# A feed-forward block of local attention and gated layers: two layers over two sequences, as four staggered passes with a guest of experts beside them

## What is computed

```python
def _layer(x, wqkv, qs, ksc, wo, lg, lb, w1, b1, w2, b2):
    h = shift_token(x)
    q, k, v = jnp.split(h @ wqkv, 3, axis=-1)          # 8 heads of 64
    q = l2norm(q) * qs
    k = l2norm(k) * ksc
    q, k = rotary_xpos(q, k)
    o = local_attention(q, k, v)                       # window 64
    x = x + o @ wo
    h = shift_token(x)
    h = (h - mu) / jnp.sqrt(var + 1e-05) * lg + lb
    a, g = jnp.split(h @ w1 + b1, 2, axis=-1)          # 341 hidden each
    x = x + (a * gelu(g)) @ w2 + b2
...
# _L1_ffn_ref: 64 experts of width 64, the 8 chosen of them weighted
h = silu(einsum('td,edf->etf', xf, W_up))
y = einsum('etf,efd->etd', h, W_down)
routed = einsum('etd,te->td', y, cw)
```

## Time and profile before

| what | value |
|---|---|
| time, median of 3 runs | 5565.12 us (5562.16 to 5575.62) |
| the profiled execution | 5573.75 us |
| its span | 5572.0 us |
| TensorE busy | 4237.3 us, 76% |
| VectorE busy | 3172.3 us, 57% |
| ScalarE busy | 2506.1 us, 45% |
| GpSimd busy | 1501.4 us, 27% |
| granted TensorE clock, mean | 0.879 |

### The profile page before, as it was taken

One profiled execution on the slowest core, in us unless ns is written; L12 is line 12 of the kernel. 1 busy time (PEld: TensorE's weight loads), 2 busy tenths in 40 slices (PEclk: granted clock), 3 DMA queues, 4 the chain that ended last, 5 costly groups with the idle time before them and its releaser, 6 DMA issues. The chain is left out here.

```text
span 5572.0 us, 51193 instructions
## 1 busy us (share of the span) xinstructions
PE 4237.3 (76%) x16034; PEld 2320.4 (42%) x16034; DVE 3172.3 (57%) x5382; ACT 2506.1 (45%) x5663; POOL 1501.4 (27%) x1096
## 2 busy tenths in 40 slices
PE   5686688787876878777886878768787787877756
PEld 3444444444533544344444434434443444444312
DVE  3323365765556555755557655575556655575576
ACT  2343344543454434634446444554346444464332
POOL 2102131531125112421215322251114312252111
PEclk7787798998998989989899889989899898999877
DMA  3020011210121110311103111121112111031122
GB/s 89 1 76 0 2 47 39 83 52 28 48 65 59 44 36 31 105 35 33 43 20 106 45 31 47 59 67 48 31 36 96 40 33 44 23 106 43 37 70 69
DMA packets 188817, 273.95 MB, mean 49 GB/s; under 512 B 23448, under 2 KB 102900, under 8 KB 188532
## 3 DMA queue, kind: packets, MB, share of 16 engines
q1 hardware_dynamic: 167652, 234.89, 13.4%
q10 hardware_dynamic: 20880, 35.52, 2.1%
HBM read 215.54 MB, written 54.79 MB: 49 GB/s over the span
## 5 line engine op out<-in xcount | busy, mean ns | idle before, releaser
L638 DVE SCALAR_TENSOR_TENSOR psum<-work,psum 128x512 f32<-128x512 f32 x528 | 366.6, 694 | 600.5 <-ACT work L576 599.4
L1463 POOL MEMSET work<- 128x256 f32 x32 | 10.0, 311 | 2323.8 <-POOLq L1265 1165.4
L1426 ACT ACTIVATE work<-psum,work 128x128 f32<-128x128 f32 (+1 forms) x1024 | 389.8, 393 | 421.6 <-DVE work L1523 421.4
L553 PE MATMUL psum<-work,w_up 128*128 128x512 f32 x1024 | 572.7, 643 | 1.5 <-DVE work L632 1.5
L558 PE MATMUL psum<-work,w_down 128*128 128x512 f32 x1024 | 551.9, 621 | 20.4 <-DVE work L645 18.2
L576 ACT ACTIVATE work<-psum 128x512 f32<-128x512 f32 x528 | 317.4, 601 | 345.2 <-PE psum L553 276.3
L1288 PE MATMUL psum<-ident,work 128*128 128x128 f32 x1024 | 187.1, 343 | 330.7 <-POOL work L1477 330.6
L1344 PE MATMUL psum<-work 128*128 128x64 f32 x3072 | 415.8, 291 | 0.0
L1344 PEld LDWEIGHTS psum<-work 128*128 128x128 f32 x3072 | 388.1, 204 | 39.0 <-issue 32.2
L1470 POOL TENSOR_TENSOR work<-work,minus_half 128x16 f32<-128x16 f32 x128 | 374.3, 2924 | 10.7
L645 DVE TENSOR_TENSOR work<-work,psum 128x512 f32<-128x512 f32 x512 | 351.4, 686 | 19.6 <-DMA work<-expert_weight_rows 2.1
(11 more groups left out here) (210 smaller groups left out, 8834.6 us busy)
## 6 DMA issues: line engine op xcount, KB each, us to landing
work<-expert_weight_rows SPq DMA_DIRECT2D x1024, 128.0 KB, 2.9
position_scores<-work SPq DMA_DIRECT2D x64, 768.0 KB, 3.5
work<-position_scores SPq DMA_DIRECT2D x64, 512.0 KB, 3.8
work<-state_readout_rows ACTq DMA_DIRECT2D x72, 256.0 KB, 3.4
cent<-state_readout_rows ACTq DMA_DIRECT2D x32, 256.0 KB, 3.6
sq<-state_readout_rows ACTq DMA_DIRECT2D x24, 256.0 KB, 3.6
rows<-in_L_attn_q SPq DMA_DIRECT2D x8, 256.0 KB, 3.7
expert_weight_rows<-work SPq DMA_DIRECT2D x16, 128.0 KB, 2.3
```

The costliest lines, as they stand in the source:

```text
L553: nc.tensor.matmul(UP, b.w_up[:, p * 128:(p + 1) * 128], self.xn, start=True, stop=True).then_inc(self.up, 1)
L638: v.scalar_tensor_tensor(out=UP, in0=self.tanh_h[p % self.turns][0:rows], scalar=1.0, in1=UP, op0=ALU.add, op1=ALU.mult).then_inc(self.sil ...
L1426: ins = s.activation(prob_of(u)[:, i, first:first + n], score_banks[:, i, first:first + n], ACT.Exp, bias=neg_max[:, t, 4 * half + i:4 * h ...
```

## The change

The two layers over two sequences become four passes (`LocalFfn`, `PASSES = DEPTH * GROUP_SEQS`): pass i is layer i // 2 of sequence i % 2. A pass has 5 rounds of projection, 8 of attention and 7 of mixing, and the rounds of neighbouring passes alternate on each engine: projection 0; attention 0 with projection 1; attention 1 with mixing 0; projection 2 with mixing 1; attention 2 with projection 3; attention 3 with mixing 2; mixing 3. I call these seven stretches A to G, and B4 is round 4 of B. All stand in one block. The guest gets 3, 5, 5, 7, 5, 5 and 8 steps in them. VectorE takes the step of a pair of experts one round after TensorE issued it. The guest's up products have one bank in place of two, and its step 2 is no longer issued in the norm block but in A.

```diff
@@ Experts @@
-    BESIDE = ((5, 6), 7)
+    BESIDE = ((6,), 7)
...
-        self.aff = bank(b, self.ups[1])[:, 0:TILES * EXPERTS].rearrange("p (t e) -> p t e", t=TILES)
-        self.norm_banks = self.ups[0:2]
+        self.aff = bank(b, self.sum_bank)[:, 0:TILES * EXPERTS].rearrange("p (t e) -> p t e", t=TILES)
+        self.norm_banks = (self.ups[0], self.sum_bank)
@@ norm_block, on TensorE, ScalarE and VectorE @@
-            beside.tensor(pe, upto=3)
@@ ffn_stage @@
-    for l in range(DEPTH):
-        ffn_layer(nc, b, prefixed(f"layer{l}"), l, beside, space, transfers if l == 0 else ([], None))
+    LocalFfn(nc, b, prefixed("passes"), space).run(beside, transfers)
@@ LocalFfn @@
+    def project_tensor(self, pe, i, k):
...
+        for n in (2 * k, 2 * k + 1):
+            out = bank(b, 4 + n % 2)
+            if 10 * i + n >= 2:
+                pe.wait_ge(self.evicted, 10 * i + n - 1)
+            if k < 3:
...
+                nc.tensor.matmul(out, b.xn[:, at:at + 128], b.wqkv[:, l, part * INNER:(part + 1) * INNER],
+                                 start=True, stop=True).then_inc(self.projected, 1)
+            else:
+                t, part = k - 3, n % 2
+                if part == 0:
+                    pe.wait_ge(self.rotated, 2 * i + t + 1)
...
+    def attend_tensor(self, pe, i, k):
+        if k == 0:
+            self.unit_scores(pe, i, 0)
+        elif k <= self.GROUPS:
+            m = k - 1
+            self.turn_probs(pe, i, m)
+            u = self.UNIT_OF[m]
+            if m in (0, 1, 2):
+                self.unit_scores(pe, i, u + 1)
+            if m >= 1:
+                self.values(pe, i, m - 1)
+        else:
+            self.values(pe, i, self.GROUPS - 1)
...
+    def attend_vector(self, dve, i, k):
+        if k == 0:
+            self.maxima(dve, i, 0)
+        elif k <= self.GROUPS:
+            m = k - 1
+            if m in (0, 1, 2):
+                self.maxima(dve, i, self.UNIT_OF[m] + 1)
+            if m % 2 == 1:
+                self.copy_probs(dve, self.nc.vector.tensor_copy, i, m, self.p_copied_v)
+            if m == 2:
+                self.scale_heads(dve, i, 0)
+        else:
+            self.scale_heads(dve, i, 1)
...
+    def run(self, beside, transfers):
+        P, A, M = self.PROJECT, self.ATTEND, self.MIX
+        due = lambda guests, k, n: (k + 1) * guests // n - k * guests // n
...
+                for k in range(A):
+                    self.attend_tensor(pe, 0, k)
+                    if k < P:
+                        self.project_tensor(pe, 1, k)
+                    beside.tensor(pe, due(5, k, A))
...
+                for k in range(A):
+                    self.attend_vector(dve, 0, k)
+                    beside.vector(dve, due(5, k - 1, A) if k else 0)
+                    if k in (1, 3):
+                        self.project_vector(dve, 1, k // 2)
...
+                for k in range(M):
+                    if k in (1, 3):
+                        self.project_vector(dve, 2, k // 2)
+                    beside.vector(dve, due(7, k - 1, M) if k else due(5, A - 1, A))
+                    self.mix_vector(dve, 1, k)
```

More of the change, by code:

```diff
@@ L1197, in _ @@
             norm.scalar(act, (0, 1), steps=(1,))
-            beside.scalar(act, upto=3)
         @block.vector
@@ L1204, in _ @@
             norm.vector(dve, dst, (0, 1), steps=(1,))
-            beside.vector(dve, upto=3)
 def ffn_stage(nc, b, stage_sem, beside, space, transfers):
@@ L1578, in _, with mix_scalar @@
-        @block.sync
-        def _(sp):
-            for dst, src in transfers[0]:
-                sp.dma_start(dst, src).then_inc(transfers[1], 16)
-            beside.sync(sp)
+                if c == 2:
+                    pe.wait_ge(self.gated, 3 * i + 3)
+                ins = nc.tensor.matmul(two[:, 0:SEQ], b.w2[0:rows, l, c], self.k_t[i % 2][0:rows, c], start=c == 0, stop=c == 2)
+            ins.then_inc(self.out, 1)
+    def mix_scalar(self, act, i, k):
+        s, b = self.nc.scalar, self.b
+        l, cols = self.where(i)
+        one, two = (bank(b, n) for n in self.mix_banks(i))
+        if k == 0:
+            act.wait_ge(self.o_turned, 2 * i + 1)
+            s.copy(self.o_t[:, :, 0:128], one.rearrange("p (j n) -> p j n", j=4)).then_inc(self.o_copied_a, 1)
+        elif k == 2:
+            act.wait_ge(self.centred, i + 1)
+            s.activation(b.sq[:, cols], two[:, 0:SEQ], ACT.Square).then_inc(self.h_squared, 1)
+        elif k == 3:
+            s.preload_act_table_set("natural_log_exp_and_others")
+            act.wait_ge(self.variance, i + 1)
+            s.activation(b.rstd[:, cols], one[:, 0:SEQ], ACT.Ln, bias=b.eps[:]).then_inc(self.logged, 1)
+            act.wait_ge(self.logged, i + 1)
+            s.activation(b.rstd[:, cols], b.rstd[:, cols], ACT.Exp, scale=-0.5).then_inc(self.inverse, 1)
+        elif k in (4, 5):
+            for c in ((0, 1), (2,))[k - 4]:
+                rows = HC[c][1]
+                act.wait_ge(self.hidden, 3 * i + c + 1)
+                s.activation(self.q_t[i % 2][0:rows, c], (one, two)[c % 2][0:rows, 0:SEQ], ACT.Gelu,
+                             bias=vec(b, (("b1_gate", c), l), rows)).then_inc(self.gelu, 1)
```

689 lines of the change are left out of this document (374 added, 315 removed).

## The result

The changed kernel takes 5725.47 us (median of 4 runs, 5717.88 to 5736.84). The kernel before, run beside it, took 5570.17. The ratio is 1.0282, with a 95% interval of 1.0256 to 1.0307. It is slower by 155 us.

A forecast was written before the change was run, and what follows sets the result against it. TensorE's work plus waits around GpSimd bounded 14 stages, mostly waits and half clock the two without a guest. +174 and -88 made +86 us on 5573.75, or 5660; with the runs' lower median 5650, range 5480 to 5800.

The forecast's parts named there:

- the likeliest case: Rival 1, as worked out: more waits in 14 stages than two give back; 5650 us, own range 5590 to 5730, chance 0.50.
- the half clock: TensorE at lower clock after waits: 1.8 us charged in B and E each, 1.0 in C and F each, 1.3 in D.
- 14 stages with a guest, without the front: Guest stages from first to last copy: 237.0 us each in place of 222.2, before the 2.4 us saved ahead.
- ahead of them, step 2 moved: Block boundary ahead of a guest stage, the front: guest's step 2 no longer holds it, 2.4 us less a stage.
- 2 stages without a guest: Same TensorE work and low clock, fewer waits: 199 us in place of 243.2, -88 us for two.
- E4: Round 4 of stretch E, not a run: as in B4, TensorE's second-tile transposes wait 5.2 us for GpSimd.
- 66 us of waits and half clock: Guest stage after the change: A 14, B and E 22.6, C and F 17.4, D 8.0, G 4, against 51 before.
- 171 us of work: TensorE's work at full clock in a guest stage: passes 110.8 us, 32 pairs 57.0, the rest about 3.
- The single bank: Round 7 waits for the pair because there is one up bank and VectorE is a round behind: 2.6 us.
- Faster: Rival 2: round 7 waits and half clock behind gaps do not come; stage 219 us, total 5400, chance 0.28.
- ScalarE late: Rival 3: loads and copies delay mixing's tanh and gelu 1.4 us at eight places; 11 us a stage, 5805, chance 0.12.
- No change: Rival 4: loss and gain cancel, with a stage of 229.7 to 232.1 us; chance 0.10.

The follow-up runs named there:

- Pair first: Changed kernel with VectorE's pair of experts ahead of the scaling of the heads in round 7 of B, C, E and F: 5559.45 us, ratio 0.9981.
- pairs away from the norm: Kernel with the three edits, the five pairs of C and of F moved to rounds 0, 1, 2, 6 and 7: 5565.45 us, ratio 0.9996.
- no lag: Changed kernel with VectorE's pair in the same round as TensorE's, at TensorE's place, not one round later: 5668.74 us, ratio 1.0159.
- three edits: Changed kernel with pair first, second tile's query/key transposes in round 6 of B and E, and their round 4 pair in round 5: 5438.55 us.
- pairs left D: Kernel with the three edits, D's pairs of rounds 1 and 3 moved to C and F: 5494.35 us, ratio 0.9847.
- the last kernel: Kernel with the three edits; in A, query sums on VectorE and guest step 2 behind the second tile's projection work: 5423.85 us, ratio 0.9734.

## Why the prediction was right

Predicted was 5650 with a range of 5480 to 5800 and 0.62 for slower; 5725 is in the range, and by 5 us in the own range of the likeliest case. The mechanism was right: each wait stands where the order in the code put it. One term of the sum, the half clock, measured twice its forecast or more, and waits that came out shorter than forecast hid much of that. In the profiled execution the terms came out so:

| term | forecast | measured |
|---|---|---|
| 14 stages with a guest, without the front | 14 x +14.8 = +207 | +271 (222.2 to 241.6 in the mean) |
| ahead of them, step 2 moved | 14 x -2.4 = -34 | -26 (gaps between the blocks' parts, 15 of them) |
| 2 stages without a guest | -88 | -91 |
| the rest | 0 | +3 |
| sum | +86 | +157 |

- **Where the waits are.** Forecast in B4 and E4 5.2 us for GpSimd, measured 5.42; in round 7 of B, C, E and F 2.6, measured 2.35; in D 1.8, 3.3 and 0.5, measured 1.60, 3.14 and 0.51; in C and F 1.5, 1.5, 1.2 and 0.9, measured 1.31, 1.29, 1.44 and 0.46. The 1.1 for GpSimd in D4 did not come, G has 2.5 in place of 4, and rounds 0 to 3 of B and E have 0.4 to 1.1 in place of 1.7.
- **The mis-sized term** is the half clock within the 66 us of waits and half clock in a stage with a guest. Taken against the same 171 us of work, the 66 us measured 68.8 and 72.3. A is 2.1 us of that in either stage: 24 forecast, 26.1 measured. I had costed the chain from VectorE to GpSimd, and not that VectorE's comparison L618 would be held up beside GpSimd's product (below); by the timeline 1.7 of the 2.1 us are that, which no run isolates. B to G were forecast at 45.1 us of waits and 6.9 of half clock. They have 38.1 us of waits and 14.6 of the rest in the first-block stage, 38.0 and 18.3 in the third-block one (their length less the waits and less 161 us of work, which is the 171 without A's 10), at a clock of 0.94 and 0.92. So the waits were 7 us too long and the half clock 8 to 11 too short. That the sum for the first-block stage came so close is luck in that part. I charged 1.8 us behind B4 and 1.0 in C, and the up product alone lost 1.06 at 2085.20. Pair first shows the price of a short wait: 7.6 us fewer of them in round 7 brought 5.9 us less busy time as well.
- **First block and third block.** The third block's stage is 4 us longer in the changed kernel, and all of it is TensorE's slower work: it is busy for 192.87 us against 188.92 with the same 856 instructions, while the waits of B to G are equal. What gives the third block the lower clock is open.

```profile
1716.40:1959.70 243.30, 192.87 (x856) 120.38 (x856) 139.72 (x254) 111.72 (x264) 55.27 (x34) 0.89 0.11 36
```

- **The stages without a guest** came at 193.2 and 199.7 against 199.
- **Tables.** ScalarE's busy time in a stage went from 99.4 to 111.4 us. The seven more loads are 9.0 us of that, as forecast (14 loads in the window, 18.0 us, against 7 and 9.0); the other 3.0 come with 13 activations and 4 copies more. The Trainium skill's drain of about 1.38 us per load (ScalarE: Activation LUTs, What ACT_TABLE_LOAD costs) is not in the traces: the activation starts 0.02 us behind the load, and the load 0.02 us behind the one before it (the tanh from 2071.43 is 0.60 us long, the next load starts at 2072.05). Taking 13 loads away gave 6.3 to 9.1 us a stage, a third to a half of their 1.28 us each. The Trainium skill's advice to batch by set (ScalarE: Activation LUTs, Table sets: the hidden batching unit) does hold here, since 122 us hang on the loads. But the run with the pairs away from the norm shows that batching which takes cover away loses.
- **The single bank** I named as one half of the reason for round 7, and that is not shown. It cost nothing in the kernel before, and in the changed one the down product behind would have waited for the same pair. What the runs show as the cause is the lag together with the order, in which the pair stands behind an instruction that waits for TensorE's last values: without the lag (no lag), or with the lag and the pair ahead of the scaling (pair first), the wait is 0.44 us in place of 2.35, each time with one bank.
- **The other cases.** *Faster* needed the round-7 waits and the clock behind them to be missing. They came. With them taken out by hand the kernel is at 5559, level with the one before and not at the 5400 of that case, which had the half clock behind the other gaps gone as well. The three edits get to 5439, but by taking out B4's and E4's waits too. *ScalarE late* lies about as near to 5725 (5805) as my own 5650 does, but its mechanism is not in the trace: the waits in C and F were 6.9 and not above the 7.7 forecast. *No change* did not occur.

Still open: what sets the clock in the third block's stages, and in E when pairs left D.

## What to carry to other kernels

When work of one engine is put a round late, look on that engine for what stands ahead of it and waits for something newer: an exchange of two neighbours was worth 166 us, and the same exchange cost 59 where a long chain hung on the neighbour. A wait that is removed uncovers the one that it hid, so two edits that gave 59 and 166 us by themselves were joined by a third that moved the pair behind the uncovered wait, and the three gave 287. Count the clock into a wait: taking 7.6 us of short waits out of a stage made it 12 to 13 us shorter. Staggering passes pays where nothing else covers a chain (42 to 49 us in each stage without a guest) and is worth little where a guest does that already (220 to 223 us with the three edits, where it was 222).

## What the runs showed of the hardware

VectorE's comparison L618 (two operands from SBUF, 128x256) took 0.42 us in each of 16 executions before. In the changed kernel its median is 2.14, as L625's is 2.02. The timelines of VectorE and GpSimd there:

```profile
1996.79 2.14 DVE L618 TENSOR_TENSOR work<-work 128x256 f32<-128x256 f32 x1
1998.96 1.22 DVE L1318 TENSOR_REDUCE work<-work 128x16 f32<-128x1024 f32 x1
...
2005.50 2.02 DVE L625 TENSOR_TENSOR work<-work 128x256 f32<-128x256 f32 x1
```

```profile
1996.75 1.90 POOL L1344 TENSOR_TENSOR work<-work 128x1024 f32<-128x1024 f32 x1
...
2005.34 1.90 POOL L1344 TENSOR_TENSOR work<-work 128x1024 f32<-128x1024 f32 x1
```

Each begins while GpSimd's product runs and ends 0.28 us after it, as if it had waited for it to end. The same holds for 14 of the 16 executions of L618 and of L625, the 14 with a guest and a host. The second tile's sums stand right behind L618, so 1.7 us of it lie on A's path. The Trainium skill (SBUF — State Buffer, SBUF: two separate sides) says that VectorE and GpSimd share a pair of ports that one instruction holds for its whole length, against VectorE's instructions with two inputs from SBUF. Beside the product L1344 the trace agrees. Beside GpSimd's power L1337, which reads SBUF as well and takes 2.93 us, it does not: all 128 executions of L1323 that begin within it take their usual 0.68 to 0.70 us, and the rotation's others are as quick as ever there too (L1324, L1325, L1329).

```profile
1992.50 2.93 POOL L1337 TENSOR_TENSOR work<-work,minus_half 128x16 f32<-128x16 f32 x1
...
1992.92 0.68 DVE L1323 TENSOR_TENSOR work<-work,rope_w 128x512 f32<-128x512 f32 x1
```

The kernel before had such hold-ups too, on other lines: 22 of the 256 executions of the rotation's L1512 took 2.12 us in place of 0.42, each begun during the product L1477. In the last kernel, where both stand behind the second tile's work, all 16 executions of each take 0.42 again:

```profile
L618 DVE TENSOR_TENSOR work<-work x16: 424/425/426, 604.2 to 5333.6; 128x256 f32<-128x256 f32 x16
...
L625 DVE TENSOR_TENSOR work<-work x16: 424/425/426, 606.7 to 5336.1; 128x256 f32<-128x256 f32 x16
```

(shortest, median and longest in ns).
